# One square and one row sum per group, behind the next copy of P1, in a Strassen-type fp32 factorization-machine layer

## The reference

```python
B, N, H, L = (2048, 512, 1024, 8)   # as called: x is 2048 x 512
s   = einsum('bn,hln->bhl', x, beta)
ssq = einsum('bn,hln->bhl', x * x, beta * beta)
fm  = 0.5 * sum(s * s - ssq, axis=-1)
y   = fm + x @ W.T + b              # 2048 x 1024
```

## Time and profile before

| | |
|---|---|
| median of 3 runs | 789.49 us (788.95 to 790.73) |
| profiled execution | 789.54 us, its span 787.8 us |
| PE busy | 774.3 us, 98% of the span |
| DVE, ACT, POOL busy | 71%, 52%, 47% |
| TensorE clock granted, mean | 0.997 |

### The profile page before, as it was taken

The page is one execution under the profiler, slowest core; times in us unless marked ns, Lnnn a source line. Parts: engine busy times, 40 slices in busy tenths (PEclk is TensorE's granted clock), DMA queues, the critical chain, the costliest instruction groups (busy, mean ns, idle before and its releaser), DMA issues. The chain is left out here.

```text
span 787.8 us, 9817 instructions
## 1 busy us (share of the span) xinstructions
PE 774.3 (98%) x3382; PEld 633.7 (80%) x3382; DVE 559.4 (71%) x646; ACT 410.2 (52%) x564; POOL 369.1 (47%) x328
## 2 busy tenths in 40 slices
PE   8999999899999999999999999999999999989998
PEld 5887878688888888888888888888888888867886
DVE  6899468976666666666666765766576656699995
ACT  5665355455554555455555555555555545553330
POOL 0133175446554654465346545653556355434443
PEclk9999999999999999999999999999999999999999
DMA  9596963085624561466046515651663166438933
GB/s 342 212 383 251 363 213 104 15 326 161 228 87 146 199 223 34 147 214 214 27 154 220 208 32 172 229 177 31 218 229 125 47 220 214 148 95 312 382 128 152
DMA packets 66738, 145.35 MB, mean 185 GB/s; under 512 B 4864, under 2 KB 41728, under 8 KB 64384
## 3 DMA queue, kind: packets, MB, share of 16 engines
q1 hardware_dynamic: 66688, 144.72, 52.0%
HBM read 102.76 MB, written 41.94 MB: 184 GB/s over the span
## 5 line engine op out<-in xcount | busy, mean ns | idle before, releaser
L443 PE MATMUL bank<-t_hi,s_hi 128*128 128x512 f32 x1116 | 436.6, 391 | 8.1 <-ACT r L593 3.7
L447 PE MATMUL bank<-t_lo,s_hi 128*128 128x512 f32 x1124 | 438.1, 390 | 0.4 <-DVE t_lo L691 0.2
L449 PE MATMUL bank<-t_hi,s_lo 128*128 128x512 f32 x1116 | 434.7, 390 | 0.0
L443 PEld LDWEIGHTS bank<-t_hi,s_hi 128*128 128x128 f32 x1116 | 209.8, 188 | 57.8 <-ACT r L593 4.5
L447 PEld LDWEIGHTS bank<-t_lo,s_hi 128*128 128x128 f32 x1124 | 211.4, 188 | 44.3 <-DVE t_lo L691 1.0
L449 PEld LDWEIGHTS bank<-t_hi,s_lo 128*128 128x128 f32 x1116 | 209.8, 188 | 43.8
L954 POOL TENSOR_TENSOR r<-r 128x512 f32<-128x512 f32 x70 | 109.7, 1567 | 261.9 <-ACT r L605 261.9
L817 DVE TENSOR_REDUCE sums<-cs 128x128 f32<-128x1024 f32 x128 | 155.4, 1215 | 69.6 <-ACT cs L624 68.7
L801 DVE TENSOR_TENSOR cs<-bank,r 128x512 f32<-128x512 f32 x70 | 48.4, 691 | 85.4 <-PE bank L449 84.9
L958 POOL TENSOR_TENSOR cs<-r 128x512 f32<-128x512 f32 x70 | 92.7, 1324 | 22.0 <-issue 17.0
L950 POOL TENSOR_TENSOR acc<-acc,bias_all 128x128 f32<-128x128 f32 x128 | 60.8, 496 | 87.2 <-DMA acc<-acc_kept 87.1
(11 more groups left out here) (53 smaller groups left out, 343.6 us busy)
## 6 DMA issues: line engine op xcount, KB each, us to landing
s_hi<-s_hi_kept SPq DMA_DIRECT2D x30, 896.0 KB, 5.2
s_lo<-s_lo_kept SPq DMA_DIRECT2D x30, 896.0 KB, 6.9
t_lo_in<-beta_p SPq DMA_DIRECT2D x16, 1024.0 KB, 7.1
s_lo_in<-x_p SPq DMA_DIRECT2D x16, 512.0 KB, 4.3
acc_kept<-cs SPq DMA_DIRECT2D x16, 512.0 KB, 5.4
acc<-acc_kept SPq DMA_DIRECT2D x64, 128.0 KB, 4.8
acc_kept<-acc SPq DMA_DIRECT2D x64, 128.0 KB, 1.8
s_hi_kept<-s_hi SPq DMA_DIRECT2D x8, 896.0 KB, 6.1
```

What stands on the lines that cost most here:

```text
L443: nc.tensor.matmul(to, s_hi[:, slot, s_op, cols], hi[:, k, :], start=start, stop=False, skip_group_check=True)
L447: nc.tensor.matmul(to, s_hi[:, slot, s_op, cols], lo[:, k, :], start=False, stop=False, skip_group_check=True)
L449: return nc.tensor.matmul(to, s_lo[:, slot, s_op, cols], hi[:, k, :], start=False, stop=stop, skip_group_check=True)
```

## The change

1. Squares: `square_12` and `square_row2` become one `square_rest` over C12, C21 and C22 (1536 columns), in the next group behind `copy_r1`. The two reductions become one over all 2048 columns, with one semaphore.
2. DVE order in groups 8 to 71: `add_c21`, steps, `add_r2`, `sum_rows`, `split_s`, `add_c12`, `sum_s`. Before it was `add_c21`, `sum_rows`, steps, `split_s`, `add_r2`, `sum_s`, `add_c12`.
3. SP order: in groups 11, 12, 69, 70 and 71 the load of x stands ahead of the store of `acc`.
4. The steps for the last pass are done in groups 65 to 68, two at a time.
5. Start: W and x lie in memory so that a partition's part is one row of 4 KB (x parts of 2 KB at the very start); the first operand of W comes in one transfer with one semaphore instead of two, and the first four products do their matmuls of the high part of x first.

```diff
@@ steps_in
+    if n + 1 == Q_PASS:
+        return {1: [1], 2: [2, 3], 3: [4, 5], 4: [6, 7]}.get(i, [])
@@ SP
-            load_x_part(0, 0, x0_front_loaded)
-            load_first(B11, b11_loaded[0], slice(0, 1))
-            load_first(B11, b11_loaded[1], slice(1, 2))
-            load_x_part(0, 1, x0_rest_loaded)
-            load_x_part(1, 0, x1_loaded)
-            load_x_part(1, 1, x1_loaded)
+            load_x_part(0, slice(0, 2), x0_front_loaded)
+            load_first(B11, b11_loaded)
+            load_x_part(0, slice(2, 4), x0_rest_loaded)
+            load_x_part(1, slice(0, 4), x1_loaded)
...
+                to = g + HALF - 1
+                if to in PREPARED:
+                    sp.wait_ge(p4_made, count(g - 1))
+                    if n == 1:
+                        sp.wait_ge(s_stored[slot_of(to)], 32)
+                    load_x(to)
                 if g == FIRST_MAIN:
                     store_v(g - 1)
                     load_acc(g)
...
@@ PE, the first four products
+            def first_product(g, place, s_op, x_split):
+
+                hi, lo = t_hi[:, 0, B11, :, :], t_lo[:, 0, B11, :, :]
+                pe.wait_ge(s_hi_ready, x_split)
+                for k in range(KP):
+                    cols = slice(k * P, (k + 1) * P)
+                    pe.wait_ge(t_hi_ready, t_split_place(0, B11, k))
+                    nc.tensor.matmul(bank(g, place), s_hi[:, g, s_op, cols], hi[:, k, :],
...
+                    pe.wait_ge(t_lo_ready, t_split_place(0, B11, k))
+                    nc.tensor.matmul(bank(g, place), s_hi[:, g, s_op, cols], lo[:, k, :],
...
+                pe.wait_ge(s_lo_ready, x_split)
+                for k in range(KP):
+                    nc.tensor.matmul(bank(g, place), s_lo[:, g, s_op, k * P:(k + 1) * P], hi[:, k, :],
@@ ACT
-            def square_12(g):
...
+            def square_rest(g):
                 act.wait_ge(c12_added, count(g))
                 act.wait_ge(c21_added, count(g))
                 act.wait_ge(c22_added, count(g))
-                nc.scalar.activation(cs[:, g % 2, 1, :, :], cs[:, g % 2, 1, :, :], ACT.Square
-                                     ).then_inc(sq2_done, 1)
+                nc.scalar.activation(squares_at(g)[:, COLS:], squares_at(g)[:, COLS:], ACT.Square
+                                     ).then_inc(squared, 1)
@@ DVE, sum_rows
+                dve.wait_ge(squared, m + 1)
+                nc.vector.tensor_reduce(sums[:, :, :].rearrange("p r h -> p (r h)"),
+                                        squares_at(g).rearrange("p (h l) -> p h l", l=L), AX_X, ALU.add
+                                        ).then_inc(rows_summed, 1)
@@ host
-        "w_p": w_columns[::-1].reshape(4, KP, P, COLS),
+        "w_p": w_columns[::-1].reshape(4, KP, P, COLS).transpose(0, 2, 1, 3),
```

More of the change, by code:

```diff
@@ L163, in fm_layer @@
         x_loaded = [sem(f"x_loaded{i}") for i in range(HALF)]
-        b11_loaded = [sem(f"b11_loaded{i}") for i in range(KP)]
+        b11_loaded = sem("b11_loaded")
         b21_loaded = sem("b21_loaded")
@@ L267, in load_x, with load_x_part @@
             def load_x(g):
[L268 to L273, removed]
+                blocks = x_at(g)[:, 0:4, :].rearrange("p b c -> p (b c)")
+                sp.dma_start(blocks, x_p[pair_of(g)]).then_inc(x_loaded[slot_of(g)], 16)
+            def load_x_part(pair, blocks, loaded):
+                sp.dma_start(s_lo_in[:, pair, blocks, :].rearrange("p b c -> p (b c)"),
+                             x_p[pair][:, 256 * blocks.start:256 * blocks.stop]).then_inc(loaded, 16)
             def store_s(g):
@@ L812, in sum_rows @@
                 dve.wait_ge(c11_taken, count(g))
-                for row in range(2):
-                    dve.wait_ge(sq12_done if row == 0 else sq2_done, m + 1)
-                    if row == 0 and m:
-                        dve.wait_ge(acc_added, m)
-                    nc.vector.tensor_reduce(
-                        sums[:, row, :].rearrange("p (c h) -> p c h", c=2),
-                        cs[:, g % 2, row, :, :].rearrange("p c (h l) -> p c h l", l=L), AX_X, ALU.add
-                        ).then_inc(row1_summed if row == 0 else row2_summed, 1)
-                dve.wait_ge(row2_summed, m + 1)
+                dve.wait_ge(squared, m + 1)
+                if m:
+                    dve.wait_ge(acc_added, m)
+                nc.vector.tensor_reduce(sums[:, :, :].rearrange("p r h -> p (r h)"),
+                                        squares_at(g).rearrange("p (h l) -> p h l", l=L), AX_X, ALU.add
+                                        ).then_inc(rows_summed, 1)
+                dve.wait_ge(rows_summed, m + 1)
                 dve.wait_ge(acc_biased, m + 1)
@@ L858, in _ @@
             sum_s(3)
-            for g in range(DIRECT, FIRST_Q):
+            for g in range(DIRECT, FIRST_MAIN):
                 if g > DIRECT:
                     add_c21(g - 1)
-                if g > FIRST_MAIN:
-                    sum_rows(g - 1)
-                if g > DIRECT:
                     for s in steps_in(g - 1):
-                        step((g - 1) // PAIRS + 1, s)
+                        step(1, s)
                 for other in groups_for(SPLIT_IN, g):
@@ L870, in _ @@
                 add_r2(g)
-                if g < FIRST_MAIN:
-                    for s in steps_in(g):
-                        sum_step(s)
+                for s in steps_in(g):
+                    sum_step(s)
                 for other in groups_for(SUMMED_IN, g):
@@ L876, in _ @@
                 add_c12(g)
+            for g in range(FIRST_MAIN, FIRST_Q):
+                add_c21(g - 1)
+                for s in steps_in(g - 1):
+                    step((g - 1) // PAIRS + 1, s)
+                add_r2(g)
+                if g > FIRST_MAIN:
+                    sum_rows(g - 1)
+                for other in groups_for(SPLIT_IN, g):
+                    split_s(other)
+                add_c12(g)
+                for other in groups_for(SUMMED_IN, g):
+                    sum_s(other)
             for g in range(FIRST_Q, GROUPS):
```

73 lines of the change are left out of this document (29 added, 44 removed).

## The result

| | before | after |
|---|---|---|
| median | 789.49 us | **785.56 us** (5 runs, 785.25 to 786.93) |
| ratio after / before | | 0.9947, 95% interval 0.9932 to 0.9962 |
| profiled execution | 789.54 us, span 787.8 | 786.93 us, span 785.1 |
| mean granted clock, profiled | 0.997 | 0.996 |

It is faster by 0.5%, where 1.0% was forecast: 785.56 for 781.8, and 0.36 above the end of the range. The profiled execution of after is its longest; the other four had a mean clock of 0.998 and 785.25 to 785.92.

A forecast was written before the change was run, and what follows sets the result against it. PE was taken as the bound, busy 774.3 of 787.8 us, so only its waits count. The terms 0.45 - 4.1 - 3.2 - 0.1 - 0.7 = -7.7 against 789.54 gave 781.8 us, range 779.8 to 785.2.

The forecast's parts named there:

- the sums of 15 now start when no sum of blocks runs: Groups 12 and 13: DVE's sums of x for group 15 miss POOL's sum of blocks; given as argument against 785.6 us.
- The walk through groups 11 to 13: Groups 11 to 13: the wait moves from P2 to P3 of 13, 0.7 us; -4.8 + 0.7 = -4.1.
- the second rival: Group 13: sums and splits meet POOL in bad order, P3 waits 2 to 2.6, clock halved (1.4); 785.6 us, chance 0.14.
- A wait of 0.7 leaves the clock alone: P3 of group 13: a 0.7 us wait does not lower the clock, if 1.35 at 700.31 did not.
- the start: First products: the third begins at 10.15 for 10.73, saving a restart: -0.7 us; -1.2 or 0 by W's landing.
- the first rival: Whole kernel: goes as forecast, small waits as they fall; 781.8 us, own range 780.0 to 783.8; chance 0.70.
- Groups 69 to 71: Refill at groups 69 to 71: load of x issues at 674.1, P3 of 71 waits 0.3; -3.5 + 0.3 = -3.2 us.
- P3 of 9: Third product of group 9: copy_r5 comes later behind the longer square, 1.50 for 1.06; +0.45 us.
- P3 of 73: Third product of group 73: its chain keeps its order, with one reduction for two; -0.1 us.
- The groups between: Groups 16 to 68: the changes hide with 2 us of cover, pace stays 9.52 us a group; zero.
- the slower case by the round trip of `acc`: Some 40 operand-loading groups: acc's trip, 1.6 longer, makes P3 wait; 0.2 a group gives 789.8, 0.5 gives 802; chance 0.05.
- The rival of a start that loses: Start: PE idle from warm-up to 6.7, clock granted at half, 1.7 lost and nothing won; 784.2 us, chance 0.08.

The follow-up runs named there:

- pool_late: After, with POOL's sum of blocks of group 13 moved behind C22 of the group: 781.95 us, ratio 0.9904.
- clock_fill: After, with 12 extra matmuls, their results overwritten, between P2 and P3 of group 13: 784.51 us, ratio 0.9929.
- 4: Also written before_xearly: before, with only the loads of x moved ahead of the stores of acc: 786.66 us, ratio 0.996.
- 10: Also written x_late: after, with the loads of x put back behind the stores of acc: 792.54 us, ratio 1.0039.
- 11: After, with the steps for the last pass in their old groups, one a group from 65 to 71: 786.1 us, ratio 0.9959.
- 6: Before, with loads of x ahead of stores of acc and POOL's sum of blocks of group 13 behind C22: 784.73 us, ratio 0.9923.
- 7: Also written all_three: after, with group 13's sum of blocks behind C22, refill casts behind P5 and P7 copies, sums of x behind C21: 782.23 us, 0.9895.
- pool_cast: After, with group 13's sum of blocks behind C22 and ACT's refill casts behind the copies of P5 and P7: 781.97 us, ratio 0.9904.
- whole_first: After, with PE's old order of matmuls in the first four products: 787.32 us, ratio 0.9955.
- cast_late: After, with ACT's cast of a refill behind the copies of P5 and P7: 782.97 us, ratio 0.9919.

## Why the prediction was wrong

**Failed: "the sums of 15 now start when no sum of blocks runs."** The walk through groups 11 to 13 gave P3 of 13 a wait of 0.7, with up to 0.7 for POOL's C22. It was 3.45. The times on DVE up to there were good (the split of 14 ended at 135.9, for 136.5 forecast), though PE was further on: group 12 started at 125.5, for 126.9, so counted from there the split was 0.8 late. What was not followed was POOL's own queue: C22 of 12 held by the split of 14 (2.96 for 1.3; up to 0.7 of this was in the walk), and the sum of blocks of 13, which needs nothing but its turn, right behind it and into the sums. The shut-out was priced at 1.9 in the second rival (chance 0.14) and cost 2.65 by `pool_late`, of which L774 makes 2.2 and L777, now beside POOL's bias additions, 0.3 (0.68 for 0.41). The rest is that the sums had begun 0.2 earlier there. The walk had the right length for DVE free of that: 0.59 in `pool_late`, for 0.7.

**Failed with it: the clock.** "A wait of 0.7 leaves the clock alone" was sound: waits of 0.6 to 1.5 at group 13 or 14 left it at 1.00 in six kernels here. With 3.45 it fell as before, for 6.9 us in the profiled execution, which lost 3.0. In the four others, by their mean clock of 0.998, it was some 3.4 us; half of that, 1.7, is the most that it can have cost, and the medians of `clock_fill` and after are 1.1 apart. The rival's 1.4 lies between.

So 2.75 (3.45 - 0.7), and 1.1 to 1.7 for the clock, less 0.6 won at the start, is +3.25 to +3.85 on 781.8: 785.05 to 785.65, for 785.56 measured. With 3.0 for the clock it is 786.95, for 786.93 in the profiled execution. The second rival's 785.6 was the number, by its own mechanism at group 13. That it fits to 0.1 is luck: its wait was 0.85 too short, its 0.85 at P3 of 71 was 0.34, and its start 0.6 too slow. (The upper sum in the first rival's own range, with 1.5 more at P3 of 13 and a start of 0, is 784.0 and not 783.8; nothing hangs on it.) Its fault was the chance of 0.14, given against the rows of the trace that showed the very collision, on the ground of a start time that hung on POOL's order, which had not been walked.

**Right, in mechanism and size.** Groups 69 to 71: -3.2. The early load alone gives 1.9 of it (4), without it the two groups lose 3.9 (10), the steps add nothing (11); the rest is the new order of ACT and DVE, the last wait of 1.4 in 4 and 6 being 0.34 here. P3 of 9: +0.4 by the longer square. P3 of 73: -0.1. The groups between: nothing, at a pace of 9.53, with C22 early and the store of `acc` 1.6 later as said; the slower case by the round trip of `acc` did not occur. The end of P4 of 68 at 674.1 was when the load was to issue: 674.83 in the trace.

**Right in sign, mis-sized: the start.** -0.7 was forecast with W's operand at 6.08, -1.2 if it landed at 5. It landed at 4.9, and -1.3 came. That landing is not steady: of the ten profiled executions with W's operand in one transfer eight have it at 4.9 to 5.3, one at 6.1, one at 7.4. The rival of a start that loses did come up in single executions (7, 11), with a low clock in 7.

The Trainium skill, "SBUF — State Buffer", section "Who interferes with whom", says that issue order decides which of DVE and GpSimd blocks. The traces agree: the sum of blocks took 4.19 when the split of 15 had come 1.18 ahead of it (`pool_late`), and 2.58, with the split at 4.21, when it came 0.24 first (`pool_cast`). The fault was that the order was not walked on both queues.

Open: why the low clock lasts 3.4 us in one execution and 6.9 in another of the same kernel, and doesn't show at all in a third, and why W's first operand lands up to 2.4 us apart. Neither was tried for by itself. `pool_late` and `pool_cast` (0.9904 both) are the best kernels here that keep every part of the change; the difference to `all_three` (0.9895) is inside the intervals.

## What to carry to other kernels

When an edit frees an engine from a wait, walk the queue of the engine that shares a resource with it too, instruction by instruction, held ones included: an instruction that has nothing to wait for but its turn starts when the one ahead of it ends, and a held one moves it. Where two parts of a change touch one queue, price each without the other: here the change without the early load of x is 3 us slower than before, and with it 4 us faster. And a wait on PE can cost more than its length once the clock falls behind it: shortening the one of 3.45 to 0.59 gave 3.6 in the medians and 5.5 in the profiled executions (`pool_late`). Where another wait follows at once the low clock may cost nothing, as in before.

## What the runs showed of the hardware

- Instructions on DVE and POOL that shut each other out pass the delay on, to and fro: `r5` + `r7` held the split of 14 (3.12 for 2.02), the split held C22 (2.96 for 1.3), and C22 moved the sum of blocks (2.58) into L774 (2.62 for 0.41). Some 5 us of delays between 132.7 and 139.8.
- In the profiled executions the granted clock fell behind every wait at group 13 of 2.5 us or more (2.5, 2.5, 3.2, 3.45, 3.8, 3.8), behind none there of 1.5 or less, and not when twelve matmuls stood in the wait. Length alone doesn't decide it: P3 of 71 in `x_late` waited 2.4 at full clock, and the start of `all_three`, with PE busy for 2.28 of 4 us in several short waits, was followed by the low one. Nor is it certain from one execution to the next: of the 39 of before in the three batches 15 have a mean clock of 1.000, of the ten of `before_xearly` four.
- In before 3.4 us at the lower level cost nothing that can be seen: in each of the three batches its executions at 0.997 (ten in all) have a mean of 789.2, and those at 1.000 (15) one of 789.4 to 789.8. Those at 0.996 or 0.995 have means of 790.9 to 791.7. In the profiled execution, at 0.997, the low clock lay under P2 of 13, and `copy_r5` came only at its end.
- Kernels with the long wait have runs apart by their clock (`whole_first` 784.7 and 785.0 at 1.000, 785.7 to 788.3 at 0.998, 788.3 and 789.1 at 0.996); `pool_late` and `pool_cast`, without it, stay within 1.7 and 0.8 us. Not all of such a spread is the clock: `cast_late` has one execution of 786.05 at 1.000, the others 782.05 to 783.45.
